# Two routed-expert stages on one Trainium2 core: loops written out, a third raw weight buffer filled by one transfer, five gather buffers, and the shared weights split a second time

## What is computed

```
x = x + 0.5 * ffn(layernorm(x))
x = x + attention(layernorm(x))
x = x + 0.5 * ffn(layernorm(x))          # the same weights again

def ffn(h):                              # E = 32 experts, K = 6 per token, hidden 256, CAP = 192
    scores = sqrt(softplus(h @ gate_w.T))
    idx    = top_k(scores + bias, 6);  w = 1.5 * scores[idx] / sum(scores[idx])
    each expert takes at most its first 192 tokens:
        y = (silu(xb @ w_gate.T) * (xb @ w_up.T)) @ w_down.T
    routed = sum over the 6 experts of w * y
    shared = clip(silu(h @ sg.T) * (h @ su.T), -10, 10) @ sd.T
    return routed + shared
```

## Time and profile before

| what | value |
|---|---|
| median of 3 runs | 1676.96 us (1675.11 to 1678.25) |
| the profiled execution | 1673.66 us, span 1671.9 us |
| front 0, expert stage 0 | 0 to 216.6 us, 218.4 to about 529 us |
| attention | to about 1141 us |
| front 1, expert stage 1 | 1143.5 to 1354.2 us, 1356.0 to 1671.9 us |
| PE, DVE, ACT, POOL busy | 1486.4, 1117.1, 1034.6, 783.2 us |
| packets of the instruction queues | q8: 45, q14: 42 (1.08 MB of 255.59 MB) |
| raw expert weights | 192 transfers of 512 KB |

### The profile page before, as it was taken

The page is one execution under the profiler, slowest core; times in us unless marked ns, Lnnn a source line. Parts: engine busy times, 40 slices in busy tenths (PEclk is TensorE's granted clock), DMA queues, the critical chain, the costliest instruction groups (busy, mean ns, idle before and its releaser), DMA issues. The chain is left out here.

```text
span 1671.9 us, 26329 instructions
## 1 busy us (share of the span) xinstructions
PE 1486.4 (89%) x8436; PEld 1241.5 (74%) x8436; DVE 1117.1 (67%) x2284; ACT 1034.6 (62%) x2108; POOL 783.2 (47%) x659
## 2 busy tenths in 40 slices
PE   5999959899895789999999999895999869989986
PEld 4877758787784678887887887774887758778875
DVE  4659848777773356766666775664649857777774
ACT  5861438777684367666666666653762527777774
POOL 0113235666663666656557555420113235566664
PEclk9999979999998799999999999997999989999998
DMA  7736369999995201111111111016555459999995
GB/s 271 239 126 207 100 207 269 251 263 273 263 263 87 67 27 39 38 64 45 45 39 57 45 39 39 26 39 219 182 172 165 130 172 250 264 263 260 261 250 101
DMA packets 113031, 255.59 MB, mean 153 GB/s; under 512 B 21200, under 2 KB 22160, under 8 KB 112816
## 3 DMA queue, kind: packets, MB, share of 16 engines
q1 hardware_dynamic: 90416, 202.59, 37.6%
q0 software_dynamic: 22528, 51.92, 14.9%
HBM read 185.70 MB, written 68.76 MB: 152 GB/s over the span
## 5 line engine op out<-in xcount | busy, mean ns | idle before, releaser
L1039 DVE TENSOR_TENSOR e_w_lo<-e_raw,e_w_hi 128x1024 fp32r<-128x1024 f32 x192 | 234.1, 1220 | 35.0 <-ACT e_w_hi L953 29.8
L1558 POOL TENSOR_SCALAR t_prob<-t_prob,t_inv 128x128 f32<-128x128 f32 (+7 forms) x128 | 111.5, 871 | 221.4 <-DVE t_inv L1463 221.4
L953 ACT ACTIVATE e_w_hi<-e_raw 128x1024 fp32r<-128x1024 f32 x192 | 202.1, 1054 | 20.9 <-PEq L271 20.9
L905 POOL DMA_INDIRECT e_xg<-htab,e_gather_idx x128 | 154.4, 1206 | 67.3 <-issue 36.7
L1129 PE MATMUL e_ps_gate<-e_xt,e_w_hi 128*128 128x384 f32 x512 | 170.1, 393 | 0.0
L356 POOL TENSOR_SCALAR d_inter<-d_inter 128x512 f32<-128x512 f32 x32 | 26.5, 827 | 269.4 <-DVE d_inter L521 269.2
L916 POOL DMA_INDIRECT out<-e_y,e_add_idx x64 | 105.2, 1644 | 100.1 <-DMA out<-e_y,e_add_idx 74.0
L1129 PE MATMUL e_ps_up<-e_xt,e_w_hi 128*128 128x384 f32 x512 | 151.9, 361 | 0.0
L916 POOL DMA_INDIRECT x_after_ffn<-e_y,e_add_idx x64 | 106.0, 1656 | 96.3 <-DMA x_after_ffn<-e_y,e_add_idx 64.6
L1358 ACT ACTIVATE t_prob<-a_wide,t_neg_max,a_q_scale 128x128 f32<-128x128 f32 (+7 forms) x128 | 106.5, 832 | 54.1 <-DVE t_neg_max L1457 53.9
L1130 PE MATMUL e_ps_gate<-e_xt,e_w_lo 128*128 128x192 f32 x512 | 135.3, 264 | 0.0
(11 more groups left out here) (223 smaller groups left out, 4585.5 us busy)
## 6 DMA issues: line engine op xcount, KB each, us to landing
e_raw<-in_w_experts SPq DMA_DIRECT2D x192, 512.0 KB
htab<-d_h SPq DMA_DIRECT2D x16, 1024.0 KB, 5.5
d_x<-in_x SPq DMA_DIRECT2D x16, 512.0 KB, 6.7
d_xs<-in_x SPq DMA_DIRECT2D x32, 256.0 KB, 3.5
x_after_ffn<-d_xs SPq DMA_DIRECT2D x32, 256.0 KB, 3.1
q_x<-x_after_ffn SPq DMA_DIRECT2D x32, 256.0 KB, 3.0
t_res<-x_after_ffn SPq DMA_DIRECT2D x32, 256.0 KB, 2.6
x_after_attention<-t_res SPq DMA_DIRECT2D x32, 256.0 KB, 2.0
```

The source lines that it names most:

```text
L905: pool.indirect_dma_start(xg[u][q][:, :], None, htab, bass.IndirectOffsetOnAxis(ap=gather_idx[u][:, q:q + 1], axis=0)).then_inc(gathered[u ...
L953: act.activation(w_hi[u][:, cols], raw[u][:, cols], ACT.Copy).then_inc(hi_ready, 1)
L1039: dve.tensor_tensor(w_lo[u][:, cols], raw[u][:, cols], w_hi[u][:, cols].bitcast(F32), ALU.subtract).then_inc(lo_ready, 1)
L1558: pool.tensor_scalar(prob[:, u, 0:width(i)], prob[:, u, 0:width(i)], inv[:, u:u + 1], 1.0, ALU.mult, ALU.mult).then_inc(p_ready, 1)
```

## The change

- The experts' loops are unrolled on all engines, and code addresses buffers by e % 2, e % 3 and e % 5.
- A third raw buffer is added. Raw weights of one expert come as one transfer of 128 rows of 12,288 bytes, issued when all three thirds of the expert three before have been split. That of expert 2 is issued when the stage begins.
- There are five pairs of gather buffers. POOL first issues gathers 0 to 4, then alternates: scatter(e), gather(e+5).
- Gathers and scatters take their indices straight from `slots`, and `weigh` takes its scale straight from `e_xg`. So `e_gather_idx`, `e_add_idx`, `e_wcol` and the POOL copies are gone.
- `k.shared_hi` and `k.shared_lo` now lie in the place of the attention weights, and front 1 loads and splits the shared weights again.

```diff
-    k.shared_hi = sb("shared_hi", [P, WALL], F32R)
-    k.shared_lo = sb("shared_lo", [P, WALL], F32R)
+    k.shared_hi, k.shared_lo = (nc.alloc_sbuf_tensor_at(f"shared_{part}", [P, WALL], F32R, offset=SBUF_END - (2 - i) * 4 * WALL)
+                                for i, part in enumerate(("hi", "lo")))
...
-                if n == 0:
-                    sp.dma_start(raw_shared[:, :], a["w_shared"]).then_inc(setup_shared, 16)
+                sp.dma_start(raw_shared[:, :], a["w_shared"]).then_inc(setup_shared, 16)
...
-                    for c in range(3):
-                        part = slice(c * THIRD, (c + 1) * THIRD)
-                        sp.dma_start(raw[u][:, part], a["w_experts"][u, :, part]).then_inc(w_loaded[u][c], 16)
+                    sp.dma_start(raw[u][:, :], a["w_experts"][u, :, :]).then_inc(w_loaded[u], 16)
...
-                        elif n == 0:
-                            pe.wait_ge(setup_lo, 2)
+                        else:
+                            pe.wait_ge(setup_lo, router_set + 1)
...
+        raw = raw + [sb("e_raw2_", [P, WALL], F32)]
...
-        gather_idx = [sb(f"e_gather_idx{u}_", [HALF, 2], U32) for u in range(2)]
-        add_idx = [sb(f"e_add_idx{u}_", [HALF, 2], U32) for u in range(2)]
-        xg = [[sb(f"e_xg{u}{q}_", [HALF, ROW], F32) for q in range(2)] for u in range(2)]
+        xg = [[sb(f"e_xg{r}{q}_", [HALF, ROW], F32) for q in range(2)] for r in range(GATHERED)]
...
             def _(sp):
-                def load_weights(e, u, from_):
-                    for c in range(3):
-                        cols = slice(c * THIRD, (c + 1) * THIRD)
-                        sp.wait_ge(lo_ready, 3 * e + c + 1)
-                        sp.dma_start(raw[u][:, cols], from_[:, cols]).then_inc(w_loaded[u][c], 16)
...
+                def load_weights(e):
+                    sp.dma_start(raw[e % 3][:, :], a["w_experts"][e, :, :]).then_inc(w_loaded[e % 3], 16)
...
+                load_weights(2)
+                for c in range(min(XS, len(attention_chunks))):
+                    sp.wait_ge(y_stored[c], 16 * ((NT - 1 - c) // XS + 1))
+                    load_chunk(c)
+                for e in range(E - 3):
+                    sp.wait_ge(lo_ready, 3 * e + 3)
+                    load_weights(e + 3)
...
+                def scatter(e):
+                    pool.wait_ge(y_ready, 2 * e + 2)
+                    if e:
                         pool.wait_ge(added, 32 * e)
-                        pool.sem_inc(y_free, 1)
-                    pool.sem_inc(seen, 1)
                     for q in range(2):
-                        pool.indirect_dma_start(acc, bass.IndirectOffsetOnAxis(ap=add_idx[u][:, q:q + 1], axis=0),
-                                                y[u][q][:, :], None, compute_op=ALU.add).then_inc(added, 16)
...
+                        row = bass.IndirectOffsetOnAxis(ap=slots[:, 2 * e + q:2 * e + q + 1], axis=0)
+                        pool.indirect_dma_start(acc, row, y[e % 2][q][:, :], None, compute_op=ALU.add).then_inc(added, 16)
+
+                for e in range(GATHERED):
+                    gather(e)
                 for u in range(XS):
                     pool.wait_ge(y_stored[u], 16 * ((NT - 1 - u) // XS + 1))
...
+                for e in range(E):
+                    scatter(e)
+                    if e + GATHERED < E:
+                        gather(e + GATHERED)
...
+                def weigh(e):
+                    if e >= 2:
+                        act.wait_ge(added, 32 * (e - 1))
+                    for q in range(2):
                         act.wait_ge(d_ready, 2 * e + q + 1)
-                        act.activation(y[u][q][:, :], ps_down[q][0:HALF, :], ACT.Copy,
-                                       scale=wcol[:, bass.ds(2 * e + q, 1)]).then_inc(y_ready, 1)
...
+                        act.activation(y[e % 2][q][:, :], ps_down[q][0:HALF, :], ACT.Copy,
+                                       scale=xg[e % GATHERED][q][:, D + e:D + e + 1]).then_inc(y_ready, 1)
```

More of the change, by code:

```diff
@@ L443, in _ @@
                     if g == 0:
[L444 to L447, removed]
+                        act.wait_ge(setup_shared, 16)
+                        for part in (slice(0, WGU), slice(WGU, WALL)):
+                            act.activation(k.shared_hi[:, part], raw_shared[:, part], ACT.Copy).then_inc(setup_hi, 1)
                         act.wait_ge(loaded, 16 * 6)
@@ L858, in routed_experts @@
         part = lambda t, c, m: t[:, 2 * c:2 * c + 2, m, :]
+        third = lambda t, c: t[:, c * THIRD:(c + 1) * THIRD]
+        high, low = (lambda bank, m=m: bank[:, :].rearrange("p (b o) -> p b o", b=FB)[:, :, m * CAP:(m + 1) * CAP]
+                     for m in range(2))
+        turned = lambda c: ps_t[c][:, 0:TC].rearrange("p (k s) -> p k s", k=2)
+        attention_chunks = []
         if n == 0:
@@ L947, in _, with split @@
             def _(act):
-                act.sem_inc(y_ready, 2)
-                def split(i, u, c):
-                    cols = slice(c * THIRD, (c + 1) * THIRD)
-                    act.wait_ge(w_loaded[u][c], 16 * i + 16)
-                    act.activation(w_hi[u][:, cols], raw[u][:, cols], ACT.Copy).then_inc(hi_ready, 1)
-                def turn(i, u):
-                    e = 2 * i + u
+                def split(e, c):
+                    act.wait_ge(w_loaded[e % 3], 16 * (e // 3) + 16)
+                    act.activation(third(w_hi[e % 2], c), third(raw[e % 3], c), ACT.Copy).then_inc(hi_ready, 1)
@@ L989, in step, with split_inner @@
[L989 to L1004 removed]
+                def split_inner(e):
+                    act.wait_ge(mul_ready, e + 1)
+                    act.activation(in_hi[e % 2][:, :], inter[e % 2][:, :], ACT.Copy).then_inc(ihi_ready, 1)
@@ L1009, in split_chunk @@
                     act.activation(hi, xs[c % XS][:, :], ACT.Copy).then_inc(att_hi, 1)
-                split(0, 0, 0)
-                split(0, 0, 1)
-                turn(0, 0)
-                split(0, 0, 2)
-                step(0, 0, behind=False)
-                pairs = len(attention_chunks) // 2 if n == 0 else 0
-                for i in range(pairs):
-                    step(i, 1)
-                    split_chunk(2 * i)
-                    step(i + 1, 0)
-                    split_chunk(2 * i + 1)
@@ L1022, in _ @@
-                with act.Fori(pairs, E // 2 - 1) as i:
-                    step(i, 1)
-                    step(i + 1, 0)
-                step(E // 2 - 1, 1, ahead=False)
-                weigh(E // 2 - 1, 1, (0, 1))
+                split(0, 0)
+                split(0, 1)
+                turn(0)
+                split(0, 2)
+                for e in range(E):
+                    ahead = e + 1 < E
+                    if ahead:
+                        turn(e + 1)
+                        split(e + 1, 0)
+                    unload_gate(e)
+                    if ahead:
+                        split(e + 1, 1)
+                    gate(e)
+                    unload_up(e)
+                    if e:
+                        weigh(e - 1)
+                    split_inner(e)
+                    if ahead:
+                        split(e + 1, 2)
+                    if 0 <= e - 1 < len(attention_chunks):
+                        split_chunk(e - 1)
```

275 lines of the change are left out of this document (94 added, 181 removed).

## The result

The changed kernel takes 1687.72 us (median of 20 runs, 1678.21 to 1695.13) against 1677.58 us (20 runs): a ratio of 1.0063, 95% interval 1.0046 to 1.0080. It is 0.6% slower, outside what such a measurement can confuse with no change, where I had forecast 1643 us and so 2% faster. Its profiled execution took 1686.05 us, span 1684.3 us, against 1673.66 and 1671.9. All medians here are of fast executions: one of e3's six (1713.68 us) fell in a second, slower state in which a program sometimes runs, and is left out.

What follows compares the result with a forecast made beforehand. The prediction took POOL's chain of scatter, landing, next scatter to bound the expert stages. Terms -33 - 1 - 2 + 1.7 = -34 us on the profiled 1673.66 gave 1639.4; with 3.3 us for the median, 1643 us, range 1612 to 1692.

Steps and rivals of the forecast that it cites:

- What the chain loses: Expert stages: weights mostly miss the scatters, so the scatter chain falls from 9.21 to 8.6 us an expert, -33 us.
- rival 2: Expert stages: big weight packets or the whole burst hold the scatters up; 1714 to 1754 us, chance 0.15.
- its milder form: Expert stages: rival 2 with half of what lies between, 9.9 us a turn, 1714 us.
- the 6.85 us: Expert stages: mean time of a scatter chain turn without weights beside it, read from the profile before.
- the 2.36 us: Expert stages: what the weights' traffic was said to add per expert to the scatter chain, 9.21 - 6.85.
- The 8.05 us: Expert stages: PE's step per expert where nothing stalls, the bound if the chain falls below it.
- Gather buffers: Expert stages: five buffers issue gathers three experts early and remove PE's 18.3 us of waits, but alone shorten nothing.
- the third buffer at 0: Expert stages: the third raw weight buffer removes no wait, as no split is late before or after; price 0.
- the copies and the code written out at 0: Expert stages: removing copies gains 0 (39 us at most); fetching unrolled code costs 0, its rival 1707 us, chance 0.03.
- Front 1: Loading and splitting the shared weights again in front 1 costs 1.7 us, bounds 0 and 4 us.
- The starts of the stages: Start of both expert stages: POOL's copies go but more weights start beside the gathers; -1 us, from -2.3 to +2.6.
- The ends: End of both expert stages: last weights come one expert sooner, so one more interval runs at 6.85; -2 us.

Runs made afterwards that it cites:

- e3: Kernel before with only the weights' transfers changed: one of 12-KB rows per expert, into its two buffers; 1696.86 us, ratio 1.0110.
- e12: Changed kernel with three 4-KB-row transfers per expert, issued on a POOL semaphore increment placed behind the gathers that follow scatter e-2; 1737.7 us, ratio 1.0383.
- e14: Changed kernel with three 4-KB-row transfers per expert, issued on a POOL semaphore increment placed behind scatter e-2 itself; 1715.6 us, ratio 1.0250.
- e9: Changed kernel, still one 12-KB-row transfer per expert, but issued only when scatter e-2 has landed; 1681.5 us, ratio 1.0027.
- e10: Changed kernel with three 4-KB-row transfers per expert, issued together when scatter e-2 has landed; 1666.5 us, ratio 0.9935.
- e2: Changed kernel with three 4-KB-row transfers per expert, all issued where it issues its single one; 1667.01 us, ratio 0.9939.
- e13: Changed kernel, one 12-KB-row transfer per expert, issued on a POOL semaphore increment placed behind the gathers that follow scatter e-2; 1738.1 us, ratio 1.0380.
- e16: Changed kernel with three 4-KB-row transfers per expert, issued when the first half of scatter e-2 has landed; 1659.3 us, ratio 0.9895.
- e7: e2 with odd experts' scatters sent to a second array with its own semaphore, their sums left out of the output; 1600.16 us, ratio 0.9553.
- e15: e2's transfers, but after the first three experts only the first third of each expert's weights is loaded; 1601.78 us, ratio 0.9564.
- e4: Changed kernel with nine gather buffers and four pairs of y buffers in the second expert stage only; 1674.97 us, ratio 0.9979.
- e1: Changed kernel with each weight buffer filled by three 4-KB-row transfers, each issued when its third is free; 1668.28 us, ratio 0.9943.
- e8: Kernel before with only the shared weights loaded and split again in front 1 and placed at the end of SBUF; 1678.11 us, ratio 1.0002.

## Why the prediction was wrong

**The step that failed** is "What the chain loses": "Now the burst of 3.8 us falls mostly in the 2 to 3 us in which no scatter is under way". I put 8.6 us an expert and -33 us there; it measured 9.54 and +17.7 us. Three things in it did not hold.

First, the burst has no fixed place in the turn. I wrote that "every step is timed by the landing", so that each transfer would be issued 4.1 us into a turn. In the second stage `e_y` is ready 5.0 us before its scatter on average, in both kernels, so `weigh` and the splits rarely wait for a landing; they follow PE, and in the changed kernel the bursts come every 8.0 us until PE stands for a gather. They were issued anywhere from 1.4 to 10.4 us into a turn of 9.5, and eight of 48 turns got two of them and took 12.0 us. The ten turns with one burst issued 4.0 to 5.0 us into them took 8.4 us on average (7.4 to 11.9), near my 8.6; but no run holds the burst there, so that it would pay is not shown. Where a run did hold the burst, it was dear: 10.2 to 10.7 us a turn for one issued 0.3 to 1.4 us into it (e12 to e14), 9.2 to 9.6 for one issued just ahead of the next scatter (e9, e10). The Trainium skill, "DMA: Bandwidth & Descriptors", section "Queues, rings and completion order", says that a transfer's semaphore increment lands only after every earlier write of that engine, in whatever queue. That e12's landing comes only as the burst runs out agrees with it, but half of the engines' time was still POOL's queue there, so no run here parts that rule from plain sharing of the engines.

Second, the one transfer of 12-KB rows. Its price was named as rival 2, and the run showed less than its milder form (9.54 us an expert, where that had 9.9): 20 us between e2 and the changed kernel, 15 us between e10 and e9, from three transfers of 4-KB rows or one of 12-KB rows. It is not a price at every moment: in e12 and e13, where the burst is issued 1.36 us into the turn and runs beside the scatter, both take the same (1737.7 and 1738.1 us). What decides that is open. The Trainium skill, the same page, section "SWDGE vs HWDGE vs iDMA", prefers packets of up to 4096 bytes and calls a packet the boundary at which an engine switches context; 4 KB had the lowest median of four lengths here, though by little against 6 and 2 KB. I weighed the packets against the earlier trace rows, which showed that they would be single, and then wrote "No row shows it" and left the sum as it was. The unknown price should have stood in the sum with its middle value.

Third, the 6.85 us were not what I took them for. I read the earlier trace rows as turns without weights; they are also turns without gathers, for POOL issued its last at 1631.09. So the 2.36 us are the price of weights and gathers together, and the chain's floor beside its gathers was never measured. That the two ends would meet at 8.6 had no run behind it: with all the bytes and one chain no run came below 8.97 us (e2, e10, e16: 8.97 to 9.33). The 8.05 us were had by opening the chain (e7) or by fewer bytes (e15).

**Gather buffers.** "A gather is issued three experts earlier than it is needed; PE's 18.3 us go" failed too. In steady state gather(e+5) stands behind scatter(e) in POOL's order. In the kernel before that was so as well: its prologue issued gathers 0 to 4 ahead of scatter 0, then gather 5, scatter 1, and its loop went on like that. The changed kernel's order, gathers 0 to 4, scatter 0, gather 5, scatter 1, is the same one: five buffers move no gather by a single place in the order. At the start of a stage they do move gathers in time: see the sizes below. PE's waits came to 28.0 us. e4 then removed them with nine gather buffers and four pairs of `e_y`. The step's other half, "This alone shortens nothing", holds for the chain, which did not move; the tail became 4.1 us shorter, and the median fell by 12.7 us, of which the larger part stays open.

**What held.** The chain as the bound, PE as its victim (e4, e7); that the weights' bytes are a part of the chain's price (e15: at least 1 us an expert for two thirds of them); the third buffer at 0: in the changed kernel ACT never waits for `e_raw`, and in e3, without that buffer, it does; the copies and the code written out at 0 for the chain: e1, which has the new code without the joined transfer, has 9.30 and 9.29 us against 9.23 and 9.20, within what two profiles differ by. Front 1 was set at +1.7 and took nothing: 1359.20 - 1159.53 = 199.67 us, and 199.92 us before (e8 agrees). Of PE's first and last records of it in the changed kernel:

```profile
1159.53 1.97 PE L706 MATMUL d_ps_t<-ident,d_h 128*128 128x128 f32 x8 [14.05 <-ACT d_h L389]
...
1358.80 0.40 PE L91 MATMUL d_ps_down<-shared_hi,d_in_lo 128*128 128x512 f32 x1
```

**Sizes.** The starts of the stages were set at -1 us. From POOL's first record of a stage to its scatter 0 it took 36.26 and 32.52 us before, and 31.17 and 27.77 us now: -9.8. The copies lay on the path there after all: in the kernel before, the gathers for experts 2 and 3 came at 234.78 and 238.75 us, after a wait of 9.24 us for DVE's `e_gather_idx`, and PE stood 2.58 us for its third turn; in the changed kernel all ten gathers are issued from 217.65 to 229.83 us and PE's third turn waits for nothing. How much of the 9.8 us is the copies, the POOL copies or the buffers is not parted. It is of the size by which e1 and e2 beat the kernel before, 8 to 10 us. The ends were set at -2 and took +2.8. The last weights are no cause of it, as they are issued at 1634.20 us, 12 us ahead of scatter 27: the scatters of experts 28 to 30 wait for `e_y`, ready only 0.3 us before them, where it had been ready 4 to 5 us before them in the old kernel. PE had fallen behind, and it bounds these turns.

## What to carry to other kernels

Where one engine issues a transfer, waits for its landing and only then issues the next, that chain has to be costed with all the traffic beside it, gathers too, and with the moment of that traffic. Ask what times a burst: if it is not the landing, the burst drifts through the turn and will sometimes fall twice into one. Adding buffers in front of such a chain moves it by nothing; opening it (a second destination) or taking bytes from beside it does. Before pieces are joined into one larger transfer, look at the rows, not only at the GB/s it reaches alone: the transfer of 12-KB rows moved 3% faster alone and cost 20 us beside scatters. And when a run is meant to move something to a certain moment, read from its trace when it came: e12 to e14 placed the burst up to 4.6 us earlier than intended.

## What the runs showed of the hardware

- A late landing costs PE twice. After a stand of 6.13 us the granted clock was 0.50 (1.2 GHz) for some 4 us of work, and the step took 10.05 us for 8.0. Over the stages the mean granted clock was 0.93 in the changed kernel and 0.97 and 0.98 before, with fewer waits but longer ones.
- A semaphore increment that stands behind indirect transfers in GpSimd's program does not wait for its records of them: in e12 SyncE was released by it 1.38 us after the first of four records began, and the last of them ended at 1454.55, 4.6 us after SyncE's issue at 1449.93.
- The same 1.5 MB cost a chain of scatters different amounts by the moment: 10.65 us a turn when issued 1.36 us into it (e12), 9.3 at the landing (e10), 9.2 at the first half's landing (e16).
- Rows of 2 KB (140857 packets in all) were no better than rows of 4 KB (113207 packets): 1672.2 and 1667.0 us.
